# The low part of a convolution's mixed weights made by GpSimd in place of VectorE

## The reference

```python
def _L0_conv_ref(x, conv1_w, conv1_b, conv2_w, conv2_b, experts_w1, experts_b1, experts_w2, experts_b2, gate_w, gate_b):
    identity = x
    pooled = x.mean(axis=(-2, -1))
    gate = jax.nn.softmax(pooled @ gate_w.T + gate_b)
    kw1 = jnp.einsum('be,eoihw->boihw', gate, experts_w1) + conv1_w
    kb1 = gate @ experts_b1 + conv1_b
    kw2 = jnp.einsum('be,eoihw->boihw', gate, experts_w2) + conv2_w
    kb2 = gate @ experts_b2 + conv2_b
    per_sample = jax.vmap(lambda xi, wi, bi: _conv2d_same(xi[None], wi, bi)[0])
    out1 = jax.nn.relu(per_sample(x, kw1, kb1))
    out2 = per_sample(out1, kw2, kb2)
    return identity + out2 * RES_SCALE
...
x = x + _L0_conv_ref(_gn(x), L0_conv_conv1_w, ...)
```

## Time and profile before

| | |
|---|---|
| median of 3 runs | 370.74 us (369.99 to 372.33) |
| profiled execution, own time | 372.14 us |
| its span | 370.3 us |
| busy: PE, DVE, ACT, POOL | 317.8, 288.6, 252.7, 192.8 us |
| share of the span: PE, DVE, ACT, POOL | 86%, 78%, 68%, 52% |
| chain that ended last, largest shares | PE 59%, DVE 15%, DMA 9%, issue 7% |
| data moved by DMA | 60.95 MB, mean 165 GB/s |

### The profile page before, as it was taken

One profiled execution on the slowest core, in us unless ns is written; L12 is line 12 of the kernel. 1 busy time (PEld: TensorE's weight loads), 2 busy tenths in 40 slices (PEclk: granted clock), 3 DMA queues, 4 the chain that ended last, 5 costly groups with the idle time before them and its releaser, 6 DMA issues.

```text
span 370.3 us, 8529 instructions
## 1 busy us (share of the span) xinstructions
PE 317.8 (86%) x2983; PEld 199.9 (54%) x2983; DVE 288.6 (78%) x651; ACT 252.7 (68%) x278; POOL 192.8 (52%) x236
## 2 busy tenths in 40 slices
PE   2327673599999998999797899999999989999993
PEld 2316442256565756575554457565657565676552
DVE  4699945688979898898787698989989888693432
ACT  1155219895968787787677587878778787965710
POOL 8039417492828383757547083837475755931000
PEclk9999969599999999999999999999999999999998
DMA  9932920688999798969995888979797996395055
GB/s 196 222 67 60 226 67 2 138 164 201 188 209 199 177 217 188 211 148 211 220 213 133 189 151 183 214 178 212 183 216 169 214 195 132 88 203 141 2 130 129
DMA packets 109387, 60.95 MB, mean 165 GB/s; under 512 B 102944, under 2 KB 105248, under 8 KB 109344
## 3 DMA queue, kind: packets, MB, share of 16 engines
q1 hardware_dynamic: 108544, 59.79, 77.5%
q10 hardware_dynamic: 608, 0.59, 0.6%
q0 software_dynamic: 192, 0.01, 0.0%
HBM read 19.47 MB, written 18.87 MB: 104 GB/s over the span
## 4 chain that ended last, share of the span: by engine, by line
PE 59%; DVE 15%; DMA 9%; issue 7%; SPq 3%; ACT 3%; POOL 2%; ACTq 0%; DVEq 0%; POOLq 0%
PE pg L390 56%; DMA wts<-wts 6%; DVE mix L660 5%; DVE wts L677 3%; DVE a L691 2%; DMA c<-a 2%; PE pg L353 2%; DVE stats L615 2%; PE pstat L373 2%; POOL a L879 1%; SPq L274 1%; DMA natural<-in_L_conv_conv_w 1%; SPq L310 1%; DVE img L707 1%; SPq L301 1%
## 5 line engine op out<-in xcount | busy, mean ns | idle before, releaser
L390 PE MATMUL pg<-a,wts 128*64 128x480 f16 (+1 forms) x1440 | 292.6, 362 | 15.8 <-DMA c<-a 6.0
L390 PE MATMUL pg<-c,wts 128*64 128x480 f16 (+1 forms) x1440 | 298.1, 366 | 0.0
L390 PEld LDWEIGHTS pg<-c,wts 128*64 128x64 f16 x1440 | 154.6, 110 | 70.2 <-issue 1.1
L390 PEld LDWEIGHTS pg<-a,wts 128*64 128x64 f16 x1440 | 155.0, 110 | 51.1 <-issue 12.8
L548 ACT ACTIVATE hid<-pg,col 128x480 f32<-128x480 f32 x80 | 52.5, 657 | 51.6 <-PE pg L390 41.6
L879 POOL TENSOR_TENSOR a<-xh,a 128x576 f16<-128x576 f32 x64 | 79.0, 1267 | 13.0 <-POOL col L887 8.5
L660 DVE SCALAR_TENSOR_TENSOR mix<-bank,gate,mix 128x386 f32<-128x386 f32 x96 | 74.0, 771 | 2.4
L860 POOL TENSOR_TENSOR col<-col,minus_half 128x1 f32<-128x1 f32 x16 | 13.5, 843 | 117.5 <-DVE col L633 117.5
L691 DVE TENSOR_TENSOR a<-hid,a 128x480 f16<-128x480 f32 x80 | 52.5, 657 | 23.1 <-ACT a L548 22.3
L564 ACT COPY c<-a 64x2352 f32<-64x2352 f32 x32 | 68.9, 2153 | 2.1 <-DVE a L691 1.9
L707 DVE SCALAR_TENSOR_TENSOR img<-pg,img 128x480 f32<-128x480 f32 (+1 forms) x80 | 48.1, 633 | 15.4 <-PE pg L390 13.1
(11 more groups left out here) (61 smaller groups left out, 143.5 us busy)
## 6 DMA issues: line engine op xcount, KB each, us to landing
c<-a SPq DMA_DIRECT2D x28, 588.0 KB, 7.1
img<-in_x SPq DMA_DIRECT2D x56, 288.0 KB, 6.9
out<-img SPq DMA_DIRECT2D x60, 180.0 KB, 3.0
out<-img SPq DMA_DIRECT2D x60, 108.0 KB, 2.3
wts<-wts SPq DMA_DIRECT2D x28, 96.0 KB, 2.6
c<-a SPq DMA_DIRECT2D x8, 294.0 KB, 5.9
img<-in_x SPq DMA_DIRECT2D x16, 144.0 KB, 5.1
out<-img SPq DMA_DIRECT2D x4, 120.0 KB, 2.1
```

The source lines that it names most:

```text
L390: last = nc.tensor.matmul(pg[g][side * 64:side * 64 + 64, at:at + nb * W].rearrange("p (b w) -> p b w", w=W), wts[s.c % WSETS][kind][:, v, ...
```

## The change

In every slot of samples 2 to 15, the low part of the weights and the two bias columns are made on POOL, behind the residual of the sample before, by `weights_low`. DVE keeps them for samples 0 and 1. RB is now made in one operation (mixed bias times 1/WS plus NBIAS), on either engine, and `residual_bias` goes. DVE's first mixture waits on `w_ok`, as it overwrites the buffer that POOL reads.

```diff
@@ mixture (DVE)
                 if e > 0:
                     dve.wait_ge(mix_step, t.number * (E - 1) + e)
+                elif t.at_least(EARLY + 1):
+                    dve.wait_ge(w_ok, t.number)
@@ biases (DVE, samples 0 and 1)
-                nc.vector.tensor_scalar(c[:, B2:B2 + 1], mixed[:, 1, :], 1.0 / WS, None, ALU.mult).then_inc(bias_ok, 1)
+                nc.vector.scalar_tensor_tensor(out=c[:, RB:RB + 1], in0=mixed[:, 1, :], scalar=1.0 / WS,
+                                               in1=c[:, NBIAS:NBIAS + 1], op0=ALU.mult, op1=ALU.add
+                                               ).then_inc(bias_ok, 1)
@@ slot (DVE)
                 run(hidden_low, s, 0, 0, 3)
-                run(biases, s, 1, 1)
-                run(weights, s, 1, 1)
                 run(hidden_low, s, 0, 0, 4)
@@ POOL
-            def residual_bias(t):
+            def weights_low(t):
+
                 c = col[t.ring]
-                pool.wait_ge(bias_ok, t.number + 1)
-                link(nc.gpsimd.tensor_tensor(c[:, RB:RB + 1], c[:, B2:B2 + 1], c[:, NBIAS:NBIAS + 1], ALU.add))
+                st = wts[t.c % WSETS][STRAIGHT]
+                mixed = mix[:, E % 2, :, TAPS:TAPS + 1]
+                pool.wait_ge(whi_ok, t.number + 1)
+                nc.gpsimd.tensor_tensor(st[:, :, LO, :], mix[:, E % 2, :, 0:TAPS], st[:, :, HI, :], ALU.subtract)
+                nc.gpsimd.tensor_scalar(c[:, B1:B1 + 1], mixed[:, 0, :], HS / WS, None, ALU.mult)
+                ins = nc.gpsimd.tensor_scalar(c[:, RB:RB + 1], mixed[:, 1, :], 1.0 / WS, c[:, NBIAS:NBIAS + 1],
+                                              ALU.mult, ALU.add)
+                ins.then_inc(w_ok, 1)
+                pool.wait_ge(w_ok, t.number + 1)

             def residual(t):
                 c = col[t.ring]
+                if early(t):
+                    pool.wait_ge(bias_ok, t.number + 1)
@@ slot (POOL)
             def slot(s):
-                run(residual_bias, s, 0, 0)
                 run(low_part, s, 1, 2, 0, PARTS)
                 run(coefficients, s, 2, 2)
                 run(residual, s, 0, 0)
-
-            schedule(slot, pool, 0, 2, 15, link, 4)
+                run(weights_low, s, 1, 2)
+
+            schedule(slot, pool, 0, 2, 15, link, 3)
```

## The result

The changed kernel takes **377.98 us** (median of 4 runs, 377.11 to 378.52) against 370.66 (now 4 runs, 369.99 to 372.33) for the kernel before on the same chip: ratio 1.0188, 95% interval 1.0149 to 1.0227. The forecast was 374.8 with a range of 369.5 to 381.5; the sign and the mechanism were right, but the step was +7.3 us where +4.1 was forecast, short by 3.2 us. The profiled execution has a span of 375.3 us and a time of 377.11.

What follows compares the result with a forecast made beforehand. A closed loop through the weights' crossing was to bound every regular turn: 16.23 + 1.45 + 2.2 = 19.88 us. Ten turns gave +3.2, sample 14 +0.9, together +4.1, so 370.74 becomes 374.8 us; range 369.5 to 381.5.

Steps and rivals of the forecast that it cites:

- The loop: PE's conv1, statistics matmul, weights on DVE, crossing by DMA, next conv1: 16.23 us plus the landing before, 1.45 more after.
- The delay of w_ok: Weights ready on POOL 1.45 us later in each turn, between a lower bound of 0.87 and an upper of 2.05.
- The landing: Time x from the second issue of the weights' crossing until it lands; taken at 2.2 us in every regular turn.
- the rival with x at 3.0: The crossing goes on meeting image load traffic, landing about 3.0 us, turns 20.7, total 383; chance 0.18.
- an x of 2.5: A landing of 2.5 us, the mix of the forecast's 2.2 and the rival's 3.0, giving 378.
- The factor of two: The low part was put at 0.83 us on POOL against 0.40 on DVE, agreeing with the skill page's 2x.
- hidden by the DMA: Turns that wait today win as much as full ones lose; 371 to 373, break-even delay 1.13 us; chance 0.27.
- The turn that crosses the loop's laps, 22.81 us: The turn from 188.60 to 211.41, held by PE stalls without a releaser, was taken to cover the delay.
- Sample 2: Taken as covered, like samples 8 and 15, each costing at most 1.45 us.
- Sample 14: PE free at 319.67, weights landing at 319.1; 1.45 us later they were to cost 0.9 us.
- the 195.57 us of the turns before: Ten regular turns of the kernel before, mean 19.56 us, subtracted from 198.8 to give +3.2 us.
- What DVE got back: Two biases and a low part, some 1.5 us in each of 14 turns, leave DVE; costed at 0.

Runs made afterwards that it cites:

- count_at_subtraction: The changed kernel with w_ok counted up by POOL's subtraction itself and the two one-column operations behind it on bias_ok; 370.47 us, 0.9954 of the kernel before.
- dve_hidden_low_ahead: The kernel before with only hidden_low group 4 put ahead of the biases and the low part, all still on DVE; 369.73 us, ratio 0.9949.
- after_again: The changed kernel run once more without an edit; 378.01 us, 1.0168 of the kernel before.
- two_columns_more: The changed kernel with two more one-column POOL operations into a spare tile, between the subtraction and B1; 383.95 us, 1.0361 of the kernel before.

## Why the prediction was right, and where its size was off

- *The loop.* Its fixed terms, 7.53 + 0.58 + 0.04 us, held to a few hundredths: turn less offset is 10.36 to 10.38 us in three kernels, landing included.
- *The delay of w_ok.* Forecast 1.45, measured 1.55. Its parts: counted from the statistics matmul the low part started 8.11 us in (forecast 156.9 - 148.71 = 8.2), the subtraction took 0.86 in place of 0.83, the one-column operations 0.22 and 0.27 in place of 0.44, and two pauses of 0.07 and 0.08 us between them had been left out. Together that is 0.1 us in each turn, 1 us in all.
- *The landing.* Forecast 2.2 in every regular turn, measured 2.15 to 2.23. The argument that long turns with a late issue leave little of the image load undone was right: one piece is mostly still under way at the issue, but it lands before the crossing would be complete. This excludes the rival with x at 3.0. The time of 378 that the prediction gives to an x of 2.5 was met by chance, since x was 2.2. Its x of 2.5 at 156.79 is that of the first transfer of the pair; that of the second was 2.3, which changes nothing in the sum.
- *The factor of two.* The prediction set 0.83 us on POOL beside 0.40 on DVE and found a factor of two confirmed. The 0.40 is only what was left of the low part after the residual; not blocked, it takes 0.56 us on DVE against 0.86 on POOL, 1.5 times as long. The sum did not rest on it.
- *The rival "hidden by the DMA".* It had its break-even at a delay of 1.13 us. count_at_subtraction has a delay of 8.99 - 8.08 = 0.91 and comes out 0.5% faster than before, with turns of 19.38 that are no longer than before; dve_hidden_low_ahead, with 0.49, likewise: the break-even is real, and the change lies beyond it.
- *The turn that crosses the loop's laps, 22.81 us.* I let it cover the delay in full. It did so only in part. The landing was 3.31 us there and PE's wait ended with it (the chain above, 199.04), and the stretch from 168.86 to 212.19, less a regular turn of 19.99, is 23.34. In after_again it was 22.99. So it cost 0.2 to 0.5 us. The image load had landed 0.25 us after the crossing's first issue there, so it does not explain this landing; what stretched it stays open.
- *Sample 2.* Taken as covered, it was so only in part. PE started its conv1 at 81.41, behind the crossing's landing (the chain above), and the turn took 21.67 us in both traces of the changed kernel, against 21.15, 20.82 and 21.15 before: 0.5 to 0.9 us.
- *Sample 14.* Forecast 0.9. PE's timeline has a wait of 0.85 us there:

```profile
324.54 0.35 PE L390 MATMUL pg<-a,wts 128*64 128x384 f16 x1 [0.85 <-DMA wts<-wts]
```

- *The mis-sized term: the 195.57 us of the turns before.* The sum was made against one execution, whose time of 372.14 was 1.5 us above the median of its set, and then the difference was carried over to the median unchanged. That execution had a long pattern of turns, the longest of three traces. With the 19.40 and 19.47 of two other traces, ten turns of 19.99 cost 5.9 and 5.2 us and not 4.3 (or the 3.2 that I forecast). Taken with 0.85 for sample 14, 0.2 to 0.5 for the lap's turn and 0.5 to 0.9 for sample 2 that is 6.8 to 8.1 us. The medians differ by 7.3 in the first comparison and 6.5 in the repeat, the two second profiled executions by 7.9. The first two differ by only 5.0: beside the long turns before, the changed kernel's first trace has its first statistics matmul 1.3 us earlier (17.3 against 18.6 us in the others of the two kernels), where no edit reaches. A kernel whose turns alternate has no single trace that stands for it, and its median was to be sized as such.
- *What DVE got back.* Forecast 0, and nothing shows otherwise: DVE's busy time went from 288.6 to 270.7 us and its waits for PE in the finishes from 13.1 to 30.5 us. The freed time lies off the loop.

## What to carry to other kernels

Before work is moved to an idle engine, ask what that engine has in front of it and when the last link of the path would be counted: here the same work on the same engine is 1.9% slower than before behind the residual and 1.2% faster ahead of it. Look at a long instruction that a second engine's work may be blocking, and try moving the blocker first; leaving the low part on DVE and delaying the residual gave the lowest median of all, though the two versions with the low part first on POOL lie within its interval. And where a loop closes through a DMA, a later issue is partly paid back by a shorter landing until the landing is at its floor, and then it costs its full size in every turn.

## What the runs showed that I had not expected

- DVE kept its hold over two two-input instructions that stood directly behind one another, and POOL's residual, which waited already, got its turn 0.5 us later (2.57 against 2.08 us). In the kernel before, where one-column operations follow the first of them, it got in earlier.
- Between POOL's subtraction and its two operations of one column there are pauses of 0.07 and 0.08 us, though none of the three waits for another. They come in every turn, on the path.
- The kernel before varies by 5.4 us (368.9 to 374.3 in 19 runs). The pattern of its turns accounts for the 1.5 us between the spans of its three traces; for the rest nothing is shown. The changed kernel had turns within some 0.1 us of each other. But equal turns don't make equal times: two_columns_more has them too, and its four runs went from 382.89 to 387.24 us.
